# Attention over heads: a part of the weighted sum goes to GpSimd, the sum gets a slot of its own, and the norm's scalars are made for eight sequences at a time

## The reference

```python
q = (x @ Wq.T).reshape(N, S, H, hd).transpose(0, 2, 1, 3)   # H = 16, hd = 8
k = ...; v = ...                                             # in the same way
att = jnp.einsum('nqhd,nkhd->nhqk', q, k)
```

## Time and profile before

| what | value |
|---|---|
| median of 3 runs | 3179.05 us (3176.43 to 3181.77) |
| the profiled execution, its own time | 3173.24 us |
| its span in the profile | 3171.5 us |
| busy in the span: PE, DVE, ACT, POOL | 2810.4, 2213.5, 1914.9, 1819.8 us |
| first instruction of the stage, last statistics in it | 1720.99 us, 2181.66 us |
| POOL's `qk`, line 1575 | 64 times, 3.676 us each |
| DVE's `ev`, line 1597 | 64 times, 2.281 us each |
| DVE's sum, line 1603 | 64 times, 2.236 us each |

### The profile page before, as it was taken

The page is one execution under the profiler, slowest core; times in us unless marked ns, Lnnn a source line. Parts: engine busy times, 40 slices in busy tenths (PEclk is TensorE's granted clock), DMA queues, the critical chain, the costliest instruction groups (busy, mean ns, idle before and its releaser), DMA issues. The chain is left out here.

```text
span 3171.5 us, 79074 instructions
## 1 busy us (share of the span) xinstructions
PE 2810.4 (89%) x26182; PEld 2315.9 (73%) x26183; DVE 2213.5 (70%) x4747; ACT 1914.9 (60%) x4303; POOL 1819.8 (57%) x2990
## 2 busy tenths in 40 slices
PE   6999997999999999499995999996789999999996
PEld 4666675888888888387774777774467777777775
DVE  4877885667666676445553999996878787878643
ACT  2555553666666666354442667674677777777762
POOL 3333333556666666425556777773667777777752
PEclk9999998999999999699997999997699999999998
DMA  5555563000000000122222000000000000000000
GB/s 151 156 143 157 157 169 107 2 5 13 14 11 13 13 12 15 68 69 74 74 74 68 1 0 0 0 0 1 1 1 5 8 5 8 5 8 5 8 5 10
DMA packets 205118, 129.51 MB, mean 41 GB/s; under 512 B 14256, under 2 KB 197528, under 8 KB 204184
## 3 DMA queue, kind: packets, MB, share of 16 engines
q1 hardware_dynamic: 196632, 108.60, 12.1%
q0 software_dynamic: 8192, 16.79, 1.7%
HBM read 34.85 MB, written 90.51 MB: 40 GB/s over the span
## 5 line engine op out<-in xcount | busy, mean ns | idle before, releaser
L445 ACT ACTIVATE a_e<-a_ps_s 128x512 f32<-128x512 f32 x256 | 138.9, 595 | 216.9 <-PE a_ps_s L371 216.9
L1575 POOL TENSOR_TENSOR a_qk<-a_qkv 128x2048 f32<-128x2048 f32 x64 | 235.3, 3676 | 57.8 <-ACT a_qkv L1550 53.6
L1508 PE MATMUL a_ps_s<-a_qk,w_ident 128*128 128x256 f32 x1024 | 236.7, 385 | 26.5 <-POOL a_qk L1575 26.4
L988 POOL TENSOR_TENSOR x_p<-x_p,x_rz 128x1232 f32<-128x1232 f32 x64 | 143.9, 2248 | 170.4 <-DVE x_rz L1097 170.4
L1508 PEld LDWEIGHTS a_ps_s<-a_qk,w_ident 128*128 128x128 f32 x1024 | 192.1, 192 | 55.9 <-issue 22.4
L524 POOL TENSOR_TENSOR a_k_bd<-a_kT,w_block 128x512 f32<-128x512 f32 x64 | 67.1, 1050 | 280.2 <-ACT a_kT L476 280.2
L1366 POOL DMA_INDIRECT f_yg<-f_rows_out,f_index x128 | 122.8, 959 | 177.7 <-DVE f_yo L1446 159.3
L547 DVE TENSOR_REDUCE a_nmax<-a_ps_s 128x4 f32<-128x512 f32 x256 | 164.0, 682 | 84.3 <-PE a_ps_s L366 84.3
L1557 ACT ACTIVATE a_r<-a_o,w_a_rows 128x128 f32<-128x128 f32 x512 | 220.8, 522 | 2.1 <-DVE a_o L1607 2.1
L2224 POOL TENSOR_TENSOR x_sq<-x_e 128x1232 f32<-128x1232 f32 x64 | 143.3, 2240 | 127.4 <-DVE x_t_sq L2383 127.3
L1104 DVE TENSOR_REDUCE x_top<-x_ps_s 128x16 f32<-128x1232 f32 x64 | 91.2, 1425 | 110.3 <-PE x_ps_s L728 110.3
(11 more groups left out here) (588 smaller groups left out, 9755.6 us busy)
## 6 DMA issues: line engine op xcount, KB each, us to landing
f_rows_in<-a_zeros SPq DMA_DIRECT2D x31, 1088.0 KB, 5.4
f_rows_out<-a_zeros SPq DMA_DIRECT2D x31, 1088.0 KB, 10.2
f_xin<-f_rows_in SPq DMA_DIRECT2D x135, 64.0 KB
f_rows_out<-f_yo SPq DMA_DIRECT2D x135, 64.0 KB
out<-x SPq DMA_DIRECT2D x16, 256.0 KB
f_raw<-in_late_f SPq DMA_DIRECT2D x2, 1408.0 KB, 6.1
w_ctx<-in_ctx SPq DMA_DIRECT2D x1, 2464.0 KB
f_rows_in<-f_xr,f_where POOLq DMA_INDIRECT x128
```

The lines of the kernel that those rows point to most:

```text
L988: nc.gpsimd.tensor_tensor(wide, wide, rz[:, :].unsqueeze(2).broadcast_to([P, HEADS, K]), ALU.mult).then_inc(p_ready, 1)
L1508: ins = nc.tensor.matmul(ps_s[u % 2][:, 0:HEADS * HEADS], c.ident[:, :], qk[:, u % 2, k, :, :], start=k == 0, stop=k == HD - 1)
L1575: nc.gpsimd.tensor_tensor(qk[:, u % 2, :, :, :], qkv[:, u, 0, :, :].unsqueeze(3).broadcast_to(full), qkv[:, u, 1, :, :].unsqueeze(2).broad ...
```

## The change

It has four parts. First, `ev` exists twice, and POOL adds the upper and the lower half (j from 0 to 7 and from 8 to 15) of the products of ten of the sixteen heads into a new tile `pairs`, 640 additions; DVE sums the other six heads over 16 products as before and the ten over 8 pairs. Second, DVE's sum and `o` move into a step SUM of their own, one slot after WEIGH, so SPREAD and LAST come one slot later as well, and the sums get a PSUM tile `ps_sums` of their own in place of the rest of the weight banks; `rz` exists twice. Third, POOL's loop has a body of eight slots, and the scalars are made for eight sequences at once in four parts, in four slots that follow each other; those of sequences 56 to 59 are done after the last slot. Fourth, ACT's `exp` waits for `ev` and `z` of two sequences before, where it waited for `o`. On POOL the new addition stands between `qk` and the bias.

```diff
+    HALF, FOLDED, EIGHT = HEADS // 2, 10, 8
-        ev = sb("ev", [P, HEADS, HD, HEADS])
+        ev = sb("ev", [P, 2, HEADS, HD, HEADS])
+        pairs = sb("pairs", [P, 2, FOLDED, HD, HALF])
...
-        TURN, PROJECT, MULTIPLY, SCORE, WEIGH, SPREAD, LAST = 1, 2, 3, 4, 5, 6, 7
+        TURN, PROJECT, MULTIPLY, SCORE, WEIGH, SUM, SPREAD, LAST = 1, 2, 3, 4, 5, 6, 7, 8
...
@@ scalar
-                    wait(act, o_ready, s - 1)
+                    wait(act, ev_done, s - 1)
+                    wait(act, z_done, s - 1)
                     nc.scalar.activation(weights_of(u), dif[:, u % 2, :, :], ACT.Exp, scale=HD ** -0.5).then_inc(exp_done, 1)
@@ gpsimd
+                if at := sl.step(WEIGH):
+                    s, u = at
+                    pool.wait_ge(ev_done, s + 1)
+                    wait(pool, sums_done, 2 * (s - 1))
+                    nc.gpsimd.tensor_tensor(pairs[:, u % 2, :, :, :], ev[:, u % 2, 0:FOLDED, :, 0:HALF], ev[:, u % 2, 0:FOLDED, :, HALF:HEADS],
+                                            ALU.add).then_inc(paired, 1)
...
-                if (at := sl.step(LAST + 1)) and at[1] % 4 == 3 and not (sl.fixed and at[0] == B - 1):
-                    s, u = at
-                    pool.wait_ge(stats_done, s + 1)
-                    scalars_of_four(c, pool, scaled, rated, s - 3, four, False, True)
-
-            run_slots(pool, slot, B, LAG)
+                if (at := sl.step(LAST + 1)) and (at[1] + 1) % EIGHT < 4:
+                    s, u = at
+                    part = (u + 1) % EIGHT
+                    first = s - part - (EIGHT - 1)
+                    if not sl.fixed or 0 <= first < B - EIGHT:
+                        if part == 0:
+                            pool.wait_ge(stats_done, s + 1)
+                        scalars_of(c, pool, scaled, rated, first, EIGHT, eight, False, True, first, (part,))
+                if sl.fixed and sl.t == B + LAG - 1:
+                    pool.wait_ge(stats_done, B - 4)
+                    scalars_of(c, pool, scaled, rated, B - EIGHT, 4, eight, False, True, B - EIGHT)
+
+            run_slots(pool, slot, B, LAG, EIGHT)
@@ vector
+                    wait(dve, paired, s - 1)
...
+                if at := sl.step(SUM):
+                    s, u = at
                     dve.wait_ge(ev_done, s + 1)
-                    nc.vector.tensor_reduce(sums_of(u), ev[:, :, :, :], AX.X, ALU.add).then_inc(sums_done, 1)
+                    nc.vector.tensor_reduce(sums[:, FOLDED:HEADS, :], ev[:, u % 2, FOLDED:HEADS, :, :], AX.X, ALU.add).then_inc(sums_done, 1)
+                    dve.wait_ge(paired, s + 1)
+                    nc.vector.tensor_reduce(sums[:, 0:FOLDED, :], pairs[:, u % 2, :, :, :], AX.X, ALU.add).then_inc(sums_done, 1)
```

More of the change, by code:

```diff
@@ L1467, in attention_over_heads @@
         top, dif = sb("top", [P, HEADS]), sb("dif", [P, 2, HEADS, HEADS])
-        z, rz = sb("z", [P, HEADS]), sb("rz", [P, HEADS])
-        ev = sb("ev", [P, HEADS, HD, HEADS])
+        z, rz = sb("z", [P, HEADS]), sb("rz", [P, 2, HEADS])
+        ev = sb("ev", [P, 2, HEADS, HD, HEADS])
+        pairs = sb("pairs", [P, 2, FOLDED, HD, HALF])
         o = sb("o", [P, 2, HEADS, HD])
@@ L1474, in attention_over_heads @@
         ps_e = [ps(f"ps_e{i}") for i in range(2)]
-        names = ("xn_ready", "xT_ps", "xT_ready", "qkv_ps", "qkv_ready", "qk_ready", "s_ps", "top_done", "dif_ready", "exp_done",
+        ps_sums = ps("ps_sums")
+        names = ("paired", "xn_ready", "xT_ps", "xT_ready", "qkv_ps", "qkv_ready", "qk_ready", "s_ps", "top_done", "dif_ready", "exp_done",
                  "z_done", "rz_done", "ev_done", "sums_done", "o_ready", "r_ready", "y_ps", "x_done", "biased")
-        (xn_ready, xT_ps, xT_ready, qkv_ps, qkv_ready, qk_ready, s_ps, top_done, dif_ready, exp_done,
+        (paired, xn_ready, xT_ps, xT_ready, qkv_ps, qkv_ready, qk_ready, s_ps, top_done, dif_ready, exp_done,
          z_done, rz_done, ev_done, sums_done, o_ready, r_ready, y_ps, x_done, biased) = (sem(n) for n in names)
         block = ctx.enter_context(nc.Block())
-        TURN, PROJECT, MULTIPLY, SCORE, WEIGH, SPREAD, LAST = 1, 2, 3, 4, 5, 6, 7
+        TURN, PROJECT, MULTIPLY, SCORE, WEIGH, SUM, SPREAD, LAST = 1, 2, 3, 4, 5, 6, 7, 8
         LAG = LAST
@@ L1484, in attention_over_heads @@
         final_in = sem("final_in")
-        four = sb("four", [P, 10, 4])
+        four, eight = sb("four", [P, 10, 4]), sb("eight", [P, 10, EIGHT])
         stats_done, scaled, rated, late_scaled, late_rated = (sem(n) for n in ("stats_done", "scaled", "rated", "late_scaled", "late_rated"))
@@ L1495, in weights_of @@
             return ps_e[u % 2][:, 0:HEADS * HEADS].rearrange("p (i j) -> p i j", i=HEADS)
-        def sums_of(u):
-            return ps_e[u % 2][:, HEADS * HEADS:HEADS * HEADS + D].rearrange("p (i d) -> p i d", i=HEADS)
+        sums = ps_sums[:, 0:D].rearrange("p (i d) -> p i d", i=HEADS)
         @block.tensor
@@ L1574, in slot @@
                     wait(pool, s_ps, s - 1)
-                    nc.gpsimd.tensor_tensor(qk[:, u % 2, :, :, :], qkv[:, u, 0, :, :].unsqueeze(3).broadcast_to(full),
-                                            qkv[:, u, 1, :, :].unsqueeze(2).broadcast_to(full), ALU.mult).then_inc(qk_ready, 1)
+                    nc.gpsimd.tensor_tensor(qk[:, u % 2, :, :, :], qkv[:, u % UNROLL, 0, :, :].unsqueeze(3).broadcast_to(full),
+                                            qkv[:, u % UNROLL, 1, :, :].unsqueeze(2).broadcast_to(full), ALU.mult).then_inc(qk_ready, 1)
+                if at := sl.step(WEIGH):
[4 more added lines that the diff above has]
+                                            ALU.add).then_inc(paired, 1)
                 if at := sl.step(TURN):
@@ L1596, in slot @@
                     dve.wait_ge(exp_done, s + 1)
-                    nc.vector.tensor_tensor(ev[:, :, :, :], weights_of(u).unsqueeze(2).broadcast_to(n),
+                    wait(dve, paired, s - 1)
+                    nc.vector.tensor_tensor(ev[:, u % 2, :, :, :], weights_of(u).unsqueeze(2).broadcast_to(n),
                                             qkv[:, u, 2, :, :].unsqueeze(1).broadcast_to(n), ALU.mult).then_inc(ev_done, 1)
@@ L1600, in slot @@
                     dve.wait_ge(z_done, s + 1)
-                    nc.vector.reciprocal(rz[:, :], z[:, :]).then_inc(rz_done, 1)
+                    nc.vector.reciprocal(rz[:, u % 2, :], z[:, :]).then_inc(rz_done, 1)
+                if at := sl.step(SUM):
+                    s, u = at
                     dve.wait_ge(ev_done, s + 1)
-                    nc.vector.tensor_reduce(sums_of(u), ev[:, :, :, :], AX.X, ALU.add).then_inc(sums_done, 1)
+                    nc.vector.tensor_reduce(sums[:, FOLDED:HEADS, :], ev[:, u % 2, FOLDED:HEADS, :, :], AX.X, ALU.add).then_inc(sums_done, 1)
+                    dve.wait_ge(paired, s + 1)
+                    nc.vector.tensor_reduce(sums[:, 0:FOLDED, :], pairs[:, u % 2, :, :, :], AX.X, ALU.add).then_inc(sums_done, 1)
                     dve.wait_ge(rz_done, s + 1)
-                    dve.wait_ge(sums_done, s + 1)
+                    dve.wait_ge(sums_done, 2 * (s + 1))
                     wait(dve, r_ready, s - 1)
-                    nc.vector.tensor_tensor(o[:, u % 2, :, :], sums_of(u), rz[:, :].unsqueeze(2).broadcast_to([P, HEADS, HD]),
+                    nc.vector.tensor_tensor(o[:, u % 2, :, :], sums, rz[:, u % 2, :].unsqueeze(2).broadcast_to([P, HEADS, HD]),
                                             ALU.mult).then_inc(o_ready, 1)
```

## The result

The changed kernel takes 3163.5 us (median of five, 3156.2 to 3166.3) against 3179.05: a ratio of 0.9946, interval 0.9932 to 0.9961. A second series gave 3159.4 against 3182.8, 0.9923 (0.9907 to 0.9940). The forecast was 3161. The profiled execution has a span of 3162.4 us, 9.1 less than that of before, yet the stage itself, from its first instruction to its last statistics, went from 460.96 to 438.38 us, 22.6 less. Both are read here.

The account below looks back on a forecast made before the run. DVE was taken to fill the 6.86 us slot. Savings of 15.0 (slots 16 to 63), 4.0 and 1.2 us, less 0.5 filling and 1.9 draining, gave -17.8: 3179.05 to 3161 us, range 3149 to 3179.

Parts of the forecast that it names:

- What comes off DVE: DVE's one reduce of 2.236 us becomes two, 0.935 and 0.805: 0.50 us less a slot, 6.86 to 6.36.
- My bound of 0.58: Upper bound of DVE's saving a slot, if the new instruction overlaps its neighbour by 0.08 us.
- The addition: POOL's new addition of 640 pairs, priced at 1.54 us from two-operand rows; low end 1.26, far end 2.0.
- The new wait: POOL's addition waits for the same slot's `ev`; chain of 14.43 us plus scalar part over three slots gives back 1.5.
- POOL level with DVE: In eight slots of the loop POOL's work would be 50.8 us against DVE's 50.9.
- Filling and drain: Stage's start and end: 0.5 us lost filling (0 to 1.5), 1.9 lost draining, the last sum standing one slot later.
- Slots 8 to 16: Slots 8 to 15 of the stage, without scalars: 8 x 0.50 = 4.0 us saved.
- 64 to 68: Slots with the last four scalar parts: 5 x 0.50 less 1.3 of chain, 1.2 us saved.
- The cheap addition: Rival, chance 0.24: POOL's addition costs 1.26 us, the chain never binds; 3154 us, or 3151 with no stall.
- the dear one: Rival, chance 0.13: short rows cost POOL, slower from about 2.2 us an addition; at 2.5 us about 3201.
- POOL as the bound: Rival, chance 0.13: at 2.0 us an addition POOL needs 54.5 to 54.9 us in eight slots; 3177.

## Why the prediction was right

- **The time and the sum.** 3161 against 3163.5 and 3159.4. That it came so close is partly luck. Inside the stage the change gave 4.8 us more than I said, 22.6 for 17.8, and some 5 us went outside the stage, where I had put nothing: 2.5 in the weights, where the clock falls sooner, and 2.5 in the last stage. Both have a cause that is open.
- **What comes off DVE** was the mis-sized term: 0.66 us a slot, not 0.50. The instruction times were right to 0.03; missing was the overlap of two sums in a row and the shorter gap before `o`. My bound of 0.58 did not reach it.
- **The addition** was right: 1.542 for 1.54, and the rows of eight cost nothing that can be seen. The Trainium skill's figure (GPSIMD Engine Reference, section 3.1), taken in proportion, gave 1.41; the trace does not agree with that use of it, since by the line of the four additions a short instruction also has its fixed 0.19 us. Carried on to the 2048 elements for which the Trainium skill has 4.497 us, the same line gives an estimate of 4.53: the proportion fails here, not the figure.
- **The new wait** was right in its links to 0.1 us (16.67 for 16.73, 16.11 for 16.23), and its removal gave 9.7 us. Its size was 2.6 us in eight slots and not 1.5, because DVE's own slot was shorter than I had it; the same 52.2 came out, since the stalled slots go by the chain. Two errors cancelled in the eight slots: DVE's saving 1.3 us too small, the stall 1.1 too small.
- **POOL level with DVE** was right for its work, 50.8 us: the kernel with the later addition takes 50.3.
- **Filling and drain.** From slot 5 to 8 there was a gain of 2.0 where I had 0.5 of loss. 1.4 of it lie in one slot, that of the earlier trace rows: 7.53 before, with 1.29 of idle time before `ev`, and 6.09 now, with 0.45. The kernel with the later addition takes 7.44 there, so this part is not DVE's shorter slot, and its cause is open; the other 0.6 us are DVE's. Slots 8 to 16 gave 5.1 (4.0), 64 to 68 2.4 (1.2): in straight code the last pieces stalled nothing. The drain cost 3.1 and not 1.9: from the last `o` on it is 1.2 longer. ACT starts the last `r` 1.98 us after `o` and not 0.32, since it is still at the `r` before and then waits 0.71 for a PE output product that took 3.75 us.
- **The rivals.** The cheap addition and the dear one fall with 1.542. POOL as the bound did not come at ten heads, where its work was level with DVE's and the chain set the pace, and did at fourteen.

## What to carry over

When an in-order engine gets a new instruction that waits for another engine, price the chain that runs through what is queued behind it, over as many slots as it spans, and compare it with that many slots, not with one. Here one slot more of distance cost nothing, as the buffer was there already, and gave another 9.7 us of stage, two fifths of what the change gave. Where work comes in bursts, ask how late the burst makes its engine. Spreading the pieces gave 8.2 us for no work saved; making them fewer was worth more here, 37.1 us even without the chain.

## What the runs showed of the hardware that was not expected

- Two DVE reduces in a row that don't depend on each other overlap by 0.09 us, and `o` starts 0.07 us on the mean after the end of a reduce of 0.81 us (0.03 to 0.13), where after one of 2.24 us it was 0.11 (0.08 to 0.21). The sum split in two took 1.69 us from its start to `o`, its durations add up to 1.71, and the one sum took 2.35 for a duration of 2.24.
- POOL's addition of two moving operands took 1.270, 1.401, 1.542 and 2.084 us for 512, 576, 640 and 896 elements, and rows of 8 cost it nothing that can be seen.
- A PE wait of 4.45 us was followed by scores at a granted clock of 0.68, 5.41 us in place of 3.72. The lone part of 40 matmuls behind the stage took 16.5 us where the clock fell between 7 and 8 us into it, and 18.6 to 19.3 where it fell between 2 and 4; a drain of 8.1 us before it was followed by the one, and one of 7.6 by the other.
